# Ternary weights with an exact first group: 23 matmuls of 24, and the output matrix's high rows on VectorE

## The reference, cut to what matters

```python
wg = w.reshape(O, g, 128)                       # 8 groups per row
scale = clip(mean(abs(wg), -1, keepdims=True), 1e-8)
q = where(wg/scale > 0.5, 1, where(wg/scale < -0.5, -1, 0))
return (q * scale).reshape(O, I)                # y = x @ that.T
```

## Time and profile before

| | us |
|---|---|
| median of 3 runs | 2347.63 (2345.82 to 2349.23) |
| the profiled execution | 2352.2 |
| its span, first to last instruction | 2350.4 |
| PE busy | 2135.3 (91%) |
| DVE busy | 1640.3 (70%) |
| ACT busy | 1143.4 (49%) |
| POOL busy | 919.3 (39%) |

### The profile page before, as it was taken

One profiled execution on the slowest core, in us unless ns is written; L12 is line 12 of the kernel. 1 busy time (PEld: TensorE's weight loads), 2 busy tenths in 40 slices (PEclk: granted clock), 3 DMA queues, 4 the chain that ended last, 5 costly groups with the idle time before them and its releaser, 6 DMA issues. The chain is left out here.

```text
span 2350.4 us, 52152 instructions
## 1 busy us (share of the span) xinstructions
PE 2135.3 (91%) x19912; PEld 1386.6 (59%) x19912; DVE 1640.3 (70%) x4559; ACT 1143.4 (49%) x2562; POOL 919.3 (39%) x855
## 2 busy tenths in 40 slices
PE   1565999999999999999999999998789998989988
PEld 1343666666666666666666666665445555555544
DVE  9997567667676676676676766655577777777764
ACT  7976433333333333333333333333666766666661
POOL 1111333333333333333333333332555565565650
PEclk9777999999999999999999999998899999999999
DMA  9976555656556555556465555558977868696852
GB/s 243 194 154 146 118 138 129 155 118 149 137 130 136 141 130 142 127 139 146 120 153 133 130 137 138 122 128 219 223 168 171 201 172 206 165 205 155 190 122 68
DMA packets 741961, 358.16 MB, mean 152 GB/s; under 512 B 688200, under 2 KB 688456, under 8 KB 741712
## 3 DMA queue, kind: packets, MB, share of 16 engines
q1 hardware_dynamic: 741712, 354.82, 64.2%
HBM read 104.11 MB, written 49.28 MB: 65 GB/s over the span
## 5 line engine op out<-in xcount | busy, mean ns | idle before, releaser
L819 POOL TENSOR_TENSOR halves<-prob,halves 128x384 f16<-128x384 f32 x256 | 234.6, 916 | 725.1 <-ACT halves L762 725.1
L62 PE MATMUL ps_j<-xT,wT 128*128 128x256 f16 x3744 | 428.3, 275 | 50.6 <-DMA wT<-rows_qkv 50.6
L87 DVE CUSTOM_DVE_ANT_0 prob<-ps_s,mask 128x128 f32<-128x128 f32 (+1 forms) x1024 | 304.6, 353 | 225.3 <-PE ps_s L77 224.2
L62 PEld LDWEIGHTS ps_j<-xT,wT 128*128 128x128 f16 x3744 | 368.8, 99 | 112.5 <-issue 50.6
L93 ACT ACTIVATE prob<-prob,negmax 128x128 f32<-128x128 f32 x512 | 202.0, 395 | 285.0 <-DVE negmax L87 284.8
L939 DVE TENSOR_TENSOR raw<-raw,cos 128x512 f32<-128x512 f32 x128 | 137.9, 1077 | 290.5 <-DMA swp<-raw 290.5
L62 PE MATMUL ps_t<-xT,wT 128*128 128x256 f16 x2400 | 270.2, 273 | 0.0
L62 PEld LDWEIGHTS ps_t<-xT,wT 128*128 128x128 f16 x2400 | 234.5, 98 | 38.2
L94 ACT ACTIVATE prob<-prob,negmax 128x256 f32<-128x256 f32 x512 | 252.9, 494 | 0.0
L1441 POOL TENSOR_TENSOR halves<-prob,halves 128x768 f16<-128x768 f32 x128 | 210.5, 1645 | 91.7 <-ACT halves L1385 91.6
L752 ACT ACTIVATE raw<-ps_j 128x512 f32<-128x512 f32 x78 | 46.4, 595 | 408.9 <-PE ps_j L62 408.9
(11 more groups left out here) (186 smaller groups left out, 3644.9 us busy)
## 6 DMA issues: line engine op xcount, KB each, us to landing
swp<-raw SPq DMA_DIRECT2D x512, 64.0 KB, 2.0
xin<-in_x SPq DMA_DIRECT2D x33, 512.0 KB, 4.2
kv_ahead<-in_ctx SPq DMA_DIRECT2D x16, 1024.0 KB, 5.5
x_kept<-after_self_attention SPq DMA_DIRECT2D x16, 1024.0 KB, 5.6
xres<-in_x SPq DMA_DIRECT2D x31, 512.0 KB, 4.1
after_self_attention<-xres SPq DMA_DIRECT2D x30, 512.0 KB, 3.3
queries<-q2T SPq DMA_DIRECT2D x30, 512.0 KB, 3.1
out<-x SPq DMA_DIRECT2D x10, 1024.0 KB, 4.6
```

The lines of the kernel that those rows point to most:

```text
L62: last = pe.matmul(out, lhs(i, a), rhs(j, a), start=a == 0 and k == 0, stop=a == n_tiles - 1 and k == 2)
L87: dve.tensor_tensor_reduce(scores[:, cols], bank[:, cols], hidden, scale, NO_SCORE, ALU.add, ALU.min, least[:, n:n + 1]).then_inc(done, 1)
L819: pool.tensor_tensor(halves[:, e, 1, :], prob[:, e], halves[:, e, 0, :], ALU.subtract).then_inc(prob_lo, 1)
```

## The change

A row's ratio is its first scale's float16 value over that scale (all times 256). All eight scales of the row are multiplied by this ratio, so that the first one is exactly a float16 number and its low part is zero: one tile of each product's low weight part falls away, and 23 matmuls of 24 are left (`exact` says which operand). The result is divided by the ratio: a factor per row of the matrix, which is per partition for queries and keys (applied by ACT at the eviction, now one instruction for queries and one for keys, instead of one for both; the 1/256 went into the rotation tables), and per column for values and the output projection. There DVE multiplies the bank in place in PSUM by 1/256 and by a row of factors (`factor_rows`, brought to all partitions by way of DRAM: three stores `store_factors` and three loads `load_factors` in SP's queue in steps -1, 4, 10 and 11). So values and output projection have one more DVE instruction of 512 columns per bank; `low_values` moves behind `maxima`, and `high_values` behind `projection` and the first weight tile on ACT.

In `ternary`, one instruction makes the scale and the thresholds; then come a reciprocal and a copy, a product, a multiplication by the ratio, and a second reciprocal. The high and low parts of the scales are made by POOL (`halves_of_scales`). ACT makes 15 row pieces instead of 16; for w_o it makes the 7 low ones only, and DVE the high ones, in one product of signs and scales per tile, which waits until the high half of the tile before has been transposed. Every transposed weight tile is 15 blocks instead of 16.

The diff, cut:

```diff
-def split_product(pe, out, lhs, rhs, n_tiles, part=None):
+def split_product(pe, out, lhs, rhs, n_tiles, part=None, exact=None):
     for a in part or range(n_tiles):
-        for k, (i, j) in enumerate(((0, 1), (1, 0), (0, 0))):
-            last = pe.matmul(out, lhs(i, a), rhs(j, a), start=a == 0 and k == 0,
-                             stop=a == n_tiles - 1 and k == 2)
+        terms = [t for t in ((0, 1), (1, 0), (0, 0)) if a > 0 or exact is None or t[exact] == 0]
+        for t in terms:
+            last = pe.matmul(out, lhs(t[0], a), rhs(t[1], a), start=a == 0 and t is terms[0],
+                             stop=a == n_tiles - 1 and t == (0, 0))
     return last
+def half_tile(i, a):
+    return a if i == 0 else DT + a - 1
...
                 if n < NQKV:
-                    sp.wait_ge(halved, 2 * n + 2)
-                    sp.dma_start_transpose(to.rearrange("p i a o -> p (i a) o"),
-                                           staged(n)[3].rearrange("p i d -> p (i d)")) \
-                        .then_inc(weights_transposed(n)[0], 16)
+                    sp.wait_ge(halved, rows_done(n))
+                    sp.dma_start_transpose(to, rows).then_inc(weights_transposed(n)[0], 16)
                 else:
-                    for i in range(2):
-                        sp.wait_ge(halved, 2 * n + i + 1)
-                        sp.dma_start_transpose(to[:, i], staged(n)[3][:, i]) \
+                    for i, (first, end) in enumerate(((0, DT), (DT, NWH))):
+                        if i == 0:
+                            sp.wait_ge(high_rows, n - NQKV + 1)
+                        else:
+                            sp.wait_ge(halved, rows_done(n))
+                        sp.dma_start_transpose(to[:, first:end], rows[:, first * P:end * P]) \
                             .then_inc(half_transposed(n, i)[0], 16)
...
-                split_product(pe, to[:, 0:T], lambda i, a: wqT[:, i, a, bass.ts(s, P)],
-                              lambda i, a: xT[:, b % 2, i, a, :], DT)
-                split_product(pe, to[:, T:2 * T], lambda i, a: wkT[:, i, a, bass.ts(s, P)],
-                              lambda i, a: xT[:, b % 2, i, a, :], DT).then_inc(j_ready, 1)
+                split_product(pe, to[:, 0:T], lambda i, a: wqT[:, half_tile(i, a), bass.ts(s, P)],
+                              lambda i, a: xT[:, b % 2, i, a, :], DT, exact=0)
...
-                for i, scale in ((0, scaleW), (1, low)):
-                    if n > NQKV:
-                        act.wait_ge(*half_transposed(n - 1, i))
-                    for g in range(NG):
-                        cols = bass.ts(g, GROUP)
-                        last = act.activation(rows[:, i, cols], sign[:, cols], ACT.Copy,
+                if n > NQKV:
+                    act.wait_ge(*half_transposed(n - 1, 1))
+                for i, scale in ((0, scaleR), (1, low)) if n < NQKV else ((1, low),):
+                    for g in range(i, NG):
+                        last = act.activation(rows[:, bass.ts(half_tile(i, g), P)],
+                                              sign[:, bass.ts(g, GROUP)], ACT.Copy,
                                               scale=scale[:, n % NS, g:g + 1])
                     last.then_inc(halved, 1)
...
-                act.activation(raw[:, g % 2].rearrange("p w n -> p (w n)"), bank(("qk", g, 0))[:],
-                               ACT.Copy, scale=1.0 / W_SCALE).then_inc(raw_done, 1)
+                t = g % NPAIR
+                if g < NPAIR:
+                    act.wait_ge(factor_done, number[1, t] + 1)
+                for w in range(2):
+                    last = act.activation(raw[:, g % 2, w], bank(("qk", g, 0))[:, bass.ts(w, T)],
+                                          ACT.Copy, scale=factor_qk[:, w, t:t + 1])
+                last.then_inc(raw_done, 1)
...
+            def halves_of_scales(n):
+                u = n % NS
+                pool.wait_ge(scales_done, n + 1)
+                pool.tensor_tensor(high[:, u, :], bounds[:, u, 0, :],
+                                   ratio[:, u:u + 1].broadcast_to([P, NG]), ALU.mult) \
+                    .then_inc(high_done, 1)
+                pool.wait_ge(high_done, n + 1)
+                pool.tensor_tensor(low[:, u, :], scaleR[:, u, :], high[:, u, :],
+                                   ALU.subtract).then_inc(low_done, 1)
             def low_tile(c):
...
             def ternary(n):
-                stage, below, sign, _ = staged(n)
+                stage, below, sign, rows = staged(n)
+                m, t = tiles[n]
                 u = n % NS
                 w = stage.rearrange("p (g i) -> p g i", g=NG)
+                def compare(to, k, side):
+                    dve.tensor_tensor(to.rearrange("p (g i) -> p g i", g=NG), w,
+                                      bounds[:, u, k, :].unsqueeze(2)
+                                      .broadcast_to([P, NG, GROUP]), side).then_inc(compared, 1)
                 dve.wait_ge(*weights_loaded(n))
                 dve.tensor_reduce(asum[:, u, :], w, AX.X, ALU.add,
                                   apply_absolute_value=True).then_inc(summed, 1)
                 dve.wait_ge(summed, n + 1)
+                if n == 0:
+                    dve.wait_ge(zeroed, 6)
                 if n >= NS:
-                    dve.wait_ge(halved, 2 * (n - NS) + 2)
-                for to, factor, bound in ((scaleW, W_SCALE, ALU.max), (high, W_SCALE, ALU.max),
-                                          (thr[:, :, 0], 0.5, ALU.max),
-                                          (thr[:, :, 1], -0.5, ALU.min)):
-                    dve.tensor_scalar(to[:, u, :], asum[:, u, :], factor / GROUP,
-                                      factor * SCALE_EPS, ALU.mult, bound).then_inc(scaled, 1)
-                dve.wait_ge(scaled, 4 * n + 4)
-                dve.tensor_tensor(low[:, u, :], scaleW[:, u, :], high[:, u, :],
-                                  ALU.subtract).then_inc(low_done, 1)
+                    dve.wait_ge(halved, rows_done(n - NS))
+                dve.scalar_tensor_tensor(
+                    bounds[:, u], asum[:, u, :].unsqueeze(1).broadcast_to([P, 3, NG]),
+                    SCALE_EPS * GROUP, parts.unsqueeze(2).broadcast_to([P, 3, NG]),
+                    ALU.max, ALU.mult).then_inc(scaled, 1)
+                dve.wait_ge(scaled, n + 1)
+                dve.reciprocal(inverse0[:, u:u + 1], bounds[:, u, 0, 0:1]).then_inc(first_done, 1)
+                dve.tensor_copy(high0[:, u:u + 1], bounds[:, u, 0, 0:1]).then_inc(first_done, 1)
+                dve.wait_ge(first_done, 2 * n + 2)
+                dve.tensor_tensor(ratio[:, u:u + 1], high0[:, u:u + 1], inverse0[:, u:u + 1],
+                                  ALU.mult).then_inc(ratio_done, 1)
+                dve.wait_ge(ratio_done, n + 1)
+                dve.tensor_scalar(scaleR[:, u, :], bounds[:, u, 0, :], ratio[:, u:u + 1], None,
+                                  ALU.mult).then_inc(scales_done, 1)
+                factor = factor_qk[:, m] if m < 2 else factor_vo[:, m - 2]
+                dve.reciprocal(factor[:, t:t + 1], ratio[:, u:u + 1]).then_inc(factor_done, 1)
+                compare(below, 2, ALU.is_lt)
                 before = n - 2 if n < NQKV else n - 1
-                for to, k, side in ((below, 1, ALU.is_lt), (sign, 0, ALU.is_gt)):
-                    if k == 0 and before >= 0 and n != NQKV:
-                        dve.wait_ge(halved, 2 * before + 2)
-                    dve.tensor_tensor(to.rearrange("p (g i) -> p g i", g=NG), w,
-                                      thr[:, u, k, :].unsqueeze(2).broadcast_to([P, NG, GROUP]),
-                                      side).then_inc(compared, 1)
+                if n > NQKV:
+                    dve.wait_ge(high_rows, n - NQKV)
+                if before >= 0 and n != NQKV:
+                    dve.wait_ge(halved, rows_done(before))
+                compare(sign, 1, ALU.is_gt)
                 dve.wait_ge(compared, 2 * n + 2)
                 dve.tensor_tensor(sign, sign, below, ALU.subtract).then_inc(signs, 1)
+                if n >= NQKV:
+                    dve.wait_ge(signs, n + 1)
+                    dve.wait_ge(high_done, n + 1)
+                    if n > NQKV:
+                        dve.wait_ge(*half_transposed(n - 1, 0))
+                    dve.tensor_tensor(rows[:, 0:D].rearrange("p (g i) -> p g i", g=NG),
+                                      sign.rearrange("p (g i) -> p g i", g=NG),
+                                      high[:, u, :].unsqueeze(2).broadcast_to([P, NG, GROUP]),
+                                      ALU.mult).then_inc(high_rows, 1)
...
+            def scaled_values(c):
+                half = c[2] % 2
+                dve.wait_ge(j_ready, ready(c))
+                dve.wait_ge(factor_in, 16 * (half + 1))
+                dve.scalar_tensor_tensor(bank(c)[:], bank(c)[:], 1.0 / W_SCALE,
+                                         factor_rows[:, 0, bass.ts(half, BANK)],
```

(65 more changed lines are left out.)

93 lines of the change are left out of this document (73 added, 20 removed).

## The result

| | before | after |
|---|---|---|
| median | 2349.48 us (10 runs, 2345.82 to 2356.57) | 2342.80 us (10 runs, 2339.77 to 2348.28) |
| ratio of the two | | 0.9970, 95% interval 0.9958 to 0.9982 |
| profiled execution, span | 2352.2, 2350.4 us | 2344.43, 2342.3 us |
| scores of step 12 of the loop start at | 285.95 | 324.50 |
| scores of step 126 start at | 1617.19 | 1607.18 |

The change is worth 6.7 us. The forecast was 18.7, so the median lies inside the range given (2312 to 2345), but little more than a third of the forecast gain came.

The account below looks back on a forecast made before the run. DVE was taken to bound the setup and PE the loop. The terms -50.8 + 12.6 + 18.0 + 1.5 = -18.7 us, from 2347.6, gave 2329 us, range 2312 to 2345.

Parts of the forecast that it names:

- TensorE's saving: Loop: fewer matmuls take 0.438 us off each step, 11.68 to 11.24 us; over 116 steps -50.8 us.
- Whether the loop can follow: Loop: rotation keeps about 0.5 us of slack in the tight steps despite DVE's extra multiplications; cost 0.
- The rival in which the loop falls behind: Loop: swap issued later, so the rotation is late; 2369 us at 1.4 us of lateness; chance 0.07.
- The q, k and v tiles: Setup: longer scale chain (+0.35) and POOL blocking (0.1) over 24 tiles, plus three banks of values; +12.6 us.
- POOL holds DVE up: Setup: POOL's two small operations block DVE in full, 0.5 not 0.1 us a tile; +9.6 us, 2339 us; chance 0.17.
- The w_o tiles: Setup: DVE's 1.2 us product per tile and a new wait for the previous tile's transposed high rows; +18.0 us.
- the rival in which that wait is short: Setup, w_o: first half lands in 3 us, product at 0.69 us; part costs about 5, time 2316 us; chance 0.18.
- The step that failed: SP's queue: factor stores and loads wait behind transposes that wait anyway; cost 0, at most 2 us each.
- the sign that the prediction had named for being wrong: Loop: the forecast is wrong if PE waits for `qk` between 300 and 1600 us.
- the end of the loop and the second half: Last two output banks and four of the second half: PE waits 0.7 us for one or two; +1.5 us.
- Nothing is gained: Setup costs 45 to 50 us, DVE work and waits both at their upper ends; about 2346 us; chance 0.08.

Follow-up runs that it names:

- e3: Changed kernel with the dropped matmul put back in every loop projection with a ternary matrix (24 of 24 again): 2392.16 us, ratio to before 1.0168.
- e8: e6 without VectorE's multiplications by the loaded factors (values and output projection scaled by a constant only): 2308.59 us, ratio to before 0.9820.
- e1: Changed kernel with dense factor stores (each partition's 4 or 8 factors side by side), VectorE reading the loaded rows with a stride: 2335.43 us, ratio to before 0.9933.
- e5: Changed kernel with dense factor stores, loaded rows put in order once by GpSimd so VectorE reads contiguously: 2330.29 us, ratio to before 0.9905.
- e6: e5 with the output matrix's high rows made by ScalarE, no product on VectorE: 2312.16 us, ratio to before 0.9832.
- e10: Changed kernel, scattered stores kept, only the output matrix's high rows given back to ScalarE: 2331.30 us, ratio to before 0.9906.
- e7: Kernel before the change with three stores of single 4-byte elements added, to a buffer nobody reads: 2367.50 us, ratio to before 1.0069.

## Why the prediction was wrong, and where it was right

**TensorE's saving: right.** 0.438 us a step, step 11.24, 0.7 us of waits in the loop. e3 measures the term at 49.4 us.

**Whether the loop can follow: right.** VectorE's scalings are worth 0.6 us of loop (e8). How thin that margin is e1 shows: with the same instructions at 1.07 us instead of 0.69, 0.38 us more each, the loop lost 6.4 us. The rival in which the loop falls behind has its mechanism, but the change stayed on this side of it.

**The q, k and v tiles: mechanism right, size too high.** The chain between sums and first comparison is 28.55 - 27.68 = 0.87 us (forecast 0.86, though its terms as they are written out add up to 0.96). GpSimd cost the tiles almost nothing: with dense stores step 4 starts at 162.90 where before it was 153.94 (e5), 9.0 us for 24 tiles and the scalings, against 12.6. That the changed kernel itself is 12.95 us late at step 4 (166.89) is luck: 4.0 of them are the first store's. Who is held up is shown by a tile after the change:

```profile
28.55 1.21 DVE L956 TENSOR_TENSOR below_qkv<-stage_qkv,bounds 128x1024 f16<-128x1024 f32 x1
```

```profile
28.65 1.17 POOL L884 TENSOR_TENSOR high<-bounds,ratio 128x8 f16<-128x8 f32 x1 [2.81 <-DVE scaleR L979]
29.90 1.06 POOL L888 TENSOR_TENSOR low<-scaleR,high 128x8 f32<-128x8 f32 x1
```

POOL's product of 8 columns takes 0.20 us where VectorE stands idle (e5, at 181.11) and 1.17 here, until VectorE's comparison ends. The one that starts second is held, and that can be VectorE: its L976, one column, 0.16 us as a rule, took 1.71 in an earlier tile:

```profile
21.02 2.16 POOL L893 TENSOR_TENSOR xh<-xres,xh 128x1024 f16<-128x1024 f32 x1 [2.56 <-ACT xh L800]
21.48 1.71 DVE L976 TENSOR_TENSOR ratio<-high,inverse 128x1 f32<-128x1 f16 x1
```

So the rival "POOL holds DVE up" had the lock right and the wrong side waiting: with the two small operations of a weight tile VectorE comes first. The Trainium skill ("SBUF — State Buffer", SBUF: two separate sides) has the lock; these rows agree with it.

**The w_o tiles: right.** Forecast +18.0 us. Between the starts of steps 4 and 9, before takes 91.34 us, e6 91.92 and e5 110.68, so the term is 19.3, of which 18.8 go with the product. Its length was forecast at 1.2 and is 1.229 us. The new wait is there as forecast, VectorE idle until the DMA of `wT`; the rival in which that wait is short is out (it is 12.3 us in e5). In the changed kernel itself steps 4 to 9 took 108.48 us, 2.2 less than in e5, though the second store falls in this stretch; why they took less isn't shown.

**The step that failed: "The factor stores and loads wait in SP's queue behind transposes that wait anyway: 0, at most 2 us each, since they stand ahead of swaps".** That sentence asked what the stores wait for, and not what waits behind them; it priced them as transfers like others in SyncE's queue. They land after 11 to 12 us, and what was issued right behind them was late by most of that: transposes on their own queue (11.70 us in place of 3.95), a plain load (12.5 in place of 4.6), and transposes on SyncE's queue when the store was on ScalarE's (8.94 in place of 3.70). It also set off the sign that the prediction had named for being wrong, PE waiting for `qk` between 300 and 1600 us: 5.38 us at 309.75, and 3.5 more in the step behind it, at the lower clock. Measured: 12.6 us by step 12 in the changed kernel (4.0 up to step 4, -2.2 from 4 to 9, 10.8 from 9 to 12, each against e5), 17.0 where the product doesn't share the wait (e10 against e6), 18.1 in the kernel before (e7).

**The sum, again.** At step 12, -1.3 us from the matmuls of three steps, +9.0 for the tiles, +19.3 for w_o, about -1.0 for the rest of the way and +12.6 for the stores make the 38.6 us of the timeline. The loop gives 48.6 back. 10.0 us are left at step 126, and 8.1 at the end of the span: the end of the loop and the second half cost 1.9, forecast 1.5. Two rivals come close, both by luck. "Nothing is gained" is nearest by its time (2346), "POOL holds DVE up" nearest by its gain (8.6 us) and by a setup of 40.2 us where 39.9 were measured (38.6 and the 1.3 saved in it). Neither names the stores, and what each puts its time on didn't happen. For the same reason it says little that the time lies inside the range, whose upper end was set for a setup made longer by other things.

## What to carry to other kernels

When a change adds a DMA, count its pieces before its bytes, and then read down the queue: the price is not paid by the one who waits for the transfer but by the next ones issued, here a transpose and the swap on the critical path, and once more by PE, which here went on at a lower clock after it had stood still. A small vector that has to go from partitions to a row is better written with each partition's elements side by side, and put in order once on chip by an engine with time to spare. And an operation moved to a busy engine is priced by its new place as well as by its length: the eight products of 1.23 us are about half of the 18 us that they cost, and the waits that come with their place are the rest.

## What the runs showed that I had not expected

- A store of 512 or 1024 elements of 4 bytes, each by itself, landed in 11.3 and 12.0 us; 128 pieces of 16 bytes took 2.9 and 128 of 32 bytes 1.9. The DMA transposes issued behind the scattered ones took 10.74 to 12.72 us to issue, in place of 3.00 to 3.95, and a store from ScalarE's queue did this to SyncE's transposes too (8.94 for two in place of 3.70). A plain load behind the third store landed after 12.5 us in place of 4.6.
- After a wait of 5.38 us in the middle of full work, PE's next step of the same work took 14.75 us at a granted clock of 0.77, in place of 11.24 at 1.00. In e10 it was 14.05 us at 0.81 after 7.33 us.
- VectorE's multiplication of a bank by a second operand in float32 took 0.69 us with that operand contiguous, 1.07 with a stride of 16 bytes and 1.08 with 32. A broadcast float16 operand made a product of 128 x 1024 take 1.23 us.
- VectorE and GpSimd hold each other up: the one that begins second waits, even for 1 or 8 columns: 0.16 us became 1.71 on VectorE, 0.20 became 1.17 on GpSimd.
